# Attention scores taken once, query-major, with the probabilities transposed on TensorE and the causal mask added by VectorE

## The reference

```python
q = proj(Wq); k = proj(Wk); v = proj(Wv)          # B, 16 heads, 512 tokens, 32 features
scores = (einsum('bhnd,bhmd->bhnm', q_r, k_r) + einsum('bhnd,bhmd->bhnm', q_i, k_i)) / sqrt(16)
scores = where(tril(512, 512), scores, -inf)
probs = softmax(scores, axis=-1)
out = concatenate([probs @ v_r, probs @ v_i], -1)
x = x + reshape(out) @ Wo
```

## Time and profile before

| | |
|---|---|
| median of 3 runs | 826.6 us (825.58 to 826.87) |
| profiled execution | 829.26 us, its span 827.4 us |
| TensorE busy | 759.1 us (92%) |
| VectorE busy | 628.8 us (76%) |
| ScalarE busy | 402.8 us (49%) |
| GpSimd busy | 489.6 us (59%) |
| TensorE clock granted, mean | 0.971 |

### The profile page before, as it was taken

How to read it: one execution, slowest core, us unless ns; L and a number is a source line. 1 busy time by engine, 2 the same in 40 slices (tenths; PEclk the granted TensorE clock), 3 DMA queues, 4 the chain that set the end, 5 groups by cost and what they waited for, 6 DMA issues and landing times.

```text
span 827.4 us, 15883 instructions
## 1 busy us (share of the span) xinstructions
PE 759.1 (92%) x5563; PEld 520.8 (63%) x5563; DVE 628.8 (76%) x1225; ACT 402.8 (49%) x760; POOL 489.6 (59%) x452
## 2 busy tenths in 40 slices
PE   3688999999999999999999999999999998998997
PEld 2565655765566556666666666665766564587995
DVE  2544555457768998899879987999798879789873
ACT  5114555555555566545646573647464546541111
POOL 5000000031966799678958786878787888976541
PEclk9658999999999999999999999999999999999997
DMA  5886656866686668566646675667566760100001
GB/s 180 111 105 82 98 78 84 135 84 84 84 135 78 90 84 134 70 91 107 90 94 90 103 93 100 90 104 95 76 87 107 100 93 8 58 14 8 32 14 38
DMA packets 47980, 70.54 MB, mean 85 GB/s; under 512 B 4897, under 2 KB 22578, under 8 KB 47922
## 3 DMA queue, kind: packets, MB, share of 16 engines
q1 hardware_dynamic: 46898, 69.52, 56.1%
q10 hardware_dynamic: 1024, 0.26, 0.1%
HBM read 14.98 MB, written 4.19 MB: 23 GB/s over the span
## 4 chain that ended last, share of the span: by engine, by line
PE 58%; DMA 15%; DVE 13%; POOL 5%; issue 4%; ACT 2%; SPq 1%; DVEq 0%; ACTq 0%; POOLq 0%
PE misc L518 21%; DMA stack_k<-k_lo 14%; PE exp_bank L518 14%; PE acc_bank L518 9%; PE max_bank L518 9%; PE sum_bank L518 3%; POOL prod L1570 3%; DVE neg_max L1201 2%; DVE seg_max L1201 2%; DVE x L1296 2%; SPq L449 1%; POOL prod L311 1%; DVE head_scores L1213 1%; DVE head_out L1213 1%; DVE ln_raw L1179 1%
## 5 line engine op out<-in xcount | busy, mean ns | idle before, releaser
L927 ACT ACTIVATE probs<-exp_bank 128x512 f32<-128x512 f32 x320 | 188.4, 592 | 204.0 <-PE exp_bank L518 201.1
L1201 DVE TENSOR_REDUCE neg_max<-max_bank 128x1 f32<-128x512 f32 (+1 forms) x192 | 130.6, 683 | 93.0 <-PE max_bank L518 92.4
L1570 POOL TENSOR_TENSOR prod<-head_probs,ctx_sb 128x256 f32<-128x256 f32 (+1 forms) x100 | 185.1, 1882 | 2.2 <-POOL head_probs L1565 0.5
L518 PE MATMUL max_bank<-stack_k,stack_q 96*128 96x384 f32 (+3 forms) x512 | 158.2, 372 | 17.2 <-DMA stack_k<-k_lo 9.1
L518 PE MATMUL acc_bank<-probs,values 128*32 128x512 f32 (+3 forms) x1024 | 157.6, 445 | 4.6 <-ACT log_sum L938 2.6
L311 POOL TENSOR_TENSOR prod<-x1n,ctx_sb 128x256 f32<-128x256 f32 (+1 forms) x104 | 158.4, 1554 | 4.3 <-ACT x1n L887 4.3
L518 PE MATMUL sum_bank<-probs,ones 128*32 128x512 f32 (+3 forms) x1024 | 156.9, 442 | 0.0
L518 PE MATMUL exp_bank<-stack_q,stack_k 97*128 97x384 f32 (+3 forms) x512 | 150.0, 355 | 2.1 <-DVE wf_lo L1171 1.3
L1512 POOL TENSOR_TENSOR ln_var<-ln_mv,eps 128x4 f32<-128x4 f32 x21 | 4.5, 213 | 198.3 <-DVE ln_mv L1187 198.3
L518 PEld LDWEIGHTS exp_bank<-stack_q,stack_k 97*128 97x128 f32 x512 | 84.1, 194 | 56.2 <-issue 28.2
L1201 DVE TENSOR_REDUCE seg_max<-max_bank 128x4 f32<-128x512 f32 x128 | 86.7, 682 | 28.2 <-PE max_bank L518 27.0
(11 more groups left out here) (181 smaller groups left out, 1360.2 us busy)
## 6 DMA issues: line engine op xcount, KB each, us to landing
stack_q<-q_hi SPq DMA_DIRECT2D x64, 256.0 KB, 5.6
stack_k<-k_hi SPq DMA_DIRECT2D x64, 256.0 KB, 9.6
stack_q<-q_lo SPq DMA_DIRECT2D x32, 256.0 KB, 7.0
stack_k<-k_lo SPq DMA_DIRECT2D x32, 256.0 KB, 10.7
x_in<-in_x SPq DMA_DIRECT2D x9, 512.0 KB, 4.7
ctx_sb<-in_ctx SPq DMA_DIRECT2D x32, 128.0 KB, 3.3
x<-in_x SPq DMA_DIRECT2D x7, 512.0 KB, 10.1
out<-y_sb SPq DMA_DIRECT2D x5, 512.0 KB, 3.3
```

The costliest lines, as they stand in the source:

```text
L518: return nc.tensor.matmul(*args, **kw)
L927: nc.scalar.activation(probs[:, (UNITS * g + n) % PTR, :], exp_bank[n % 2][:, :], ACT.Exp, scale=SCALE).then_inc(exp_done, 1)
L1201: vec.tensor_reduce(o, v, axis=AX_X, op=ALU.max, negate=True).then_inc(max_taken, 1)
L1570: last = gp.tensor_tensor(pv_prod[:, COFF[j]:COFF[j + 1]].rearrange("p (q d k) -> p q d k", q=4, k=keys), head_probs[:, 4 * j:4 * j + 4, N ...
```

## The change

Stages B and C become one. Scores are computed once, query-major, 96 rows, no mask matmul, into three rotating banks (`score_bank`). VectorE takes a unit strip by strip with tensor_tensor_reduce: it adds a bf16 causal mask, writes the masked scores back to the bank, and keeps the smallest (q carries the factor -SCALE, so this is the negated maximum). ScalarE takes Exp strip by strip with scale -1, that minimum as a bias on every partition, and an accumulated row sum. TensorE transposes the four 128-column blocks of the unit into one of two turn banks, three units later (LAG = 3), ScalarE copies them to probs_t, and `attend` runs once for a group, four heads side by side, with the values alone. The row sums come from ScalarE; VectorE inverts them (`invert_sums`), ScalarE widens them (`widen_inverses`), four matmuls with the identity turn them (`spread_inverses`), and `normalise` multiplies. The matmuls with ones, Ln, the two Exp(-log), the turning of the maxima and its DMA are gone. Stage A is now one group ahead (it was three), with two slots; the batch loop is written out whole, without registers. The work of the head attention, the other layer norms, the feed-forward and the tail stays, some of it at another unit n.

```diff
-    SLOTS = 4
+    SLOTS = 2
-    PTR = 4
+    RING = 4
+    LAG = 3
...
-        max_bank = [psum(f"max_bank{n}", [P, T]) for n in range(2)]
-        exp_bank = [psum(f"exp_bank{n}", [P, T]) for n in range(2)]
+        score_bank = [psum(f"score_bank{n}", [P, T]) for n in range(3)]
+        turn_bank = [psum(f"turn_bank{n}", [P, T]) for n in range(2)]
...
-            return {"C": group(0), "B": group(2), "A": group(3), "M": group(1), "N": group(-1)}
+            return {"C": group(0), "A": group(1), "N": group(-1)}
...
+            def score_unit(n, slot):
+
+                wait(pe, exp_done, n_unit.up() - 3)
+                bank = score_bank[(n_unit.total - 1) % 3]
+                for h, blk, at, width in QUERY_UNITS[n]:
+                    last = mm(bank[:, at:at + width], stack_q[0:STACK, slot, h, blk * P:(blk + 1) * P],
+                              stack_k[0:STACK, slot, h, 0:width], start=True, stop=True, skip_group_check=True)
+                last.then_inc(scored, 1)
+
+            def turn_unit():
+
+                pe.wait_ge(exp_done, n_turned.up())
+                wait(pe, probs_kept, n_turned.total - 2)
+                unit = n_turned.total - 1
+                for j in range(NT):
+                    last = nc.tensor.transpose(turn_bank[unit % 2][:, j * P:(j + 1) * P],
+                                               probs[:, unit % RING, j * P:(j + 1) * P], ident[:, :])
+                last.then_inc(turned, 1)
+
+            def attend(group):
+
+                pe.wait_ge(probs_kept, UNITS * n_group.up())
+                wait(pe, acc_saved, n_group.total - 1)
...
+                for k, (blk, row, c0, c1, q0) in enumerate(VALUE_PARTS):
+                    for h in range(G):
+                        last = mm(acc_bank[h * D:(h + 1) * D, q0:q0 + c1 - c0], values[:, group, blk, h * D:(h + 1) * D],
+                                  probs_t[:, h, row, c0:c1], start=(k == 0), stop=(k == len(VALUE_PARTS) - 1),
+                                  skip_group_check=True)
...
+            def spread_inverses():
+
+                pe.wait_ge(inv_spread, n_group.total)
+                bank = take(1, attn_ready, r_attn)
+                for t in range(NT):
+                    last = mm(bank[:, t * P:(t + 1) * P], inv_wide[:, t, :], ident[:, :], start=True, stop=True)
...
+            def exponential(n, group):
+
+                act.wait_ge(max_taken, n_unit.up())
+                unit = n_unit.total - 1
+                wait(act, turned, n_unit.total - RING)
...
+                for h, blk, at, width in QUERY_UNITS[n]:
+                    last = nc.scalar.activation(probs[:, unit % RING, at:at + width],
+                                                score_bank[unit % 3][:, at:at + width], ACT.Exp,
+                                                bias=neg_max[:, ring, h, blk:blk + 1], scale=-1.0,
+                                                accum_out=row_sum[:, ring, h, blk:blk + 1])
+                last.then_inc(exp_done, 1)
...
+                for h, blk, at, width in QUERY_UNITS[n]:
+                    v = bank[:, at:at + width]
+                    last = vec.tensor_tensor_reduce(v, v, causal[:, T - width:T], 1.0, 3.0e38, ALU.add, ALU.min,
+                                                    neg_max[:, ring, h, blk:blk + 1])
+                last.then_inc(max_taken, 1)
```

More of the change, by code:

```diff
@@ L32, with __init__ @@
 class Count:
-    def __init__(self, turn, per_batch):
-        self.turn, self.per_batch, self.total = turn, per_batch, 0
+    def __init__(self):
+        self.total = 0
     def up(self, n=1):
         self.total += n
-        return self.now()
+        return self.total
     def now(self, back=0):
[L46 to L78, removed]
+        return self.total - back
 def wait(eng, sem, value):
-    if not isinstance(value, int) or value > 0:
+    if value > 0:
         eng.wait_ge(sem, value)
[L87 to L95, removed]
 def decoder_layer(nc, x, ctx_in, wq, wk, wv, wo, ffn_w, ffn_bias, ffn_a, ffn_b, out):
@@ L833, in _ @@
             pe.wait_ge(const_ready, 1)
-            turn.batches(pe, body, N_BATCH)
+            for i in range(-1, N_BATCH):
+                body(i)
             pe.wait_ge(setup_act, 2)
-            attend((8, 9), NG - 1, UNITS * (NG - 1))
+            for n in range(LAG):
+                turn_unit()
+            attend(NG - 1)
+            spread_inverses()
             last_projection_most()
@@ new lines, in keep_turned @@
+            def keep_turned(n):
+                act.wait_ge(turned, n_kept.up())
+                unit = n_kept.total - 1
+                if n == 0:
+                    wait(act, pv_done, unit // UNITS)
+                src = turn_bank[unit % 2][:, :]
+                place = turned_place(n)
+                if n < 2 * G:
+                    src = src.rearrange("p (b q) -> p b q", q=P)
+                else:
+                    src = src.rearrange("p (h b q) -> p h b q", b=2, q=P)
+                copy(place, src).then_inc(probs_kept, 1)
@@ L923, in body @@
                         if st["C"]:
-                            act.wait_ge(exp_scored, n_exp.up())
-                            wait(act, pv_done, n_exp.now(PTR) if turn.reg is not None or n_exp.total > PTR else 0)
-                            nc.scalar.activation(probs[:, (UNITS * g + n) % PTR, :], exp_bank[n % 2][:, :],
-                                                 ACT.Exp, scale=SCALE).then_inc(exp_done, 1)
+                            exponential(n, st["C"][1])
+                        if (i, g) == (-1, 3) and n == 3:
+                            other_weights()
@@ L1448, in _ @@
             last.then_inc(w_lo_ready, 1)
-            turn.batches(dve, body, N_BATCH)
+            for i in range(-1, N_BATCH):
+                body(i)
+            invert_sums(NG - 1)
             end_vector_scores(2)
-            last_normalise()
+            normalise(NG - 1)
             end_first_tile()
```

601 lines of the change are left out of this document (243 added, 358 removed).

## The result

The changed kernel takes 928.87 us (median of 4 runs, 927.21 to 929.92), the kernel before 826.15 in the same session: a ratio of 1.124, 95% interval 1.122 to 1.126. That is 103 us slower. The forecast was 848 with a range of 803 to 910, so the sign was right and the size far off.

A forecast was written before the change was run, and what follows sets the result against it. TensorE bounds the kernel, VectorE close behind. Start 32.5, batches 0 and 1 80 and 82, five batches 467.5, last 82, final units 3 and tail 101.7 sum to 848.7, taken as 848 us; range 803 to 910.

The forecast's parts named there:

- the sign: Whole kernel: slower, chance 0.68; faster 0.27, same 0.05.
- I leave VectorE about the idle time it has now: VectorE in a middle batch: idle time stays near 10.3 us, rounded to 9.8, giving 93.5 us instead of 86.2.
- Before, a late Exp did not hold up VectorE's maxima: Scores before the change: a late Exp left VectorE's maxima undelayed; afterwards late waits go round the engines; no size given.
- VectorE's 83.7 us: VectorE's work in a middle batch: 75.9 us less 28.3 removed, plus strips, read-outs and inversions; bounds 78.6 and 95.2.
- The extra eight microseconds: VectorE in a middle batch: the added eight microseconds come from cutting units into strips, not from the mask itself.
- ScalarE's 78 us: ScalarE's work in a middle batch: 32.0 us removed; copies, strip exponentials and row sums added; between 68 and 92.
- TensorE's 72.7: TensorE's work in a middle batch: 83.0 us, minus 29.9 removed, plus 19.6 for transposes and small matmuls.
- Start and light batches: Span's start: 32.5 us to the first score, 26 us lead gone; batches 0 and 1 take 80 and 82 us.
- The ring as forecast: Rival: engines wait in one ring of scores, exponentials and transposes, VectorE bound; about 848 us; chance 0.40.
- ScalarE joins the bound: Rival: row sums cost a full small instruction; ScalarE 89 to 92 us, batch 102, total 905; chance 0.20.
- The gain case: Rival: VectorE's read-outs hide and bank slack suffices; batch 83.5 us, total 783; decides at 89 a batch; chance 0.28.
- The clock rival: Rival: waits in every batch put TensorE at its lower clock half the time; 955 us; chance 0.12.

The follow-up runs named there:

- d1: Changed kernel with four moves: coefficients a group later, transposes ahead of the projection, inverses spread a unit later, attend behind unit 3's transposes; 829.10 us, ratio 0.999.
- b2: Changed kernel with three moves: coefficients a group later, transposes ahead of the projection, inverses spread a unit later; 839.38 us, ratio 1.009.
- the run with whole banks: Changed kernel with each unit's bank taken whole, one strip a unit; 910.49 us, ratio 1.097.
- the fifth buffer: Changed kernel with four moves of instruction order, and five probability buffers in place of four; 829.40 us, ratio 0.997.
- the mended kernels: Changed kernel with three moves of instruction order (839.38 us, ratio 1.009), or with attend behind unit 3's transposes as a fourth (824.93 us, ratio 0.994).
- c4: Kernel before with VectorE's next-input statistics in later units and GpSimd's coefficients in the same group, ahead of the head attention's products; 859.41 us, ratio 1.031.

## Why the prediction was wrong

The sign was right largely by luck: the forecast had it above all from 8 us more work on VectorE in a batch, and VectorE's work did not grow. The size failed at one step.

- **The step that failed** is "I leave VectorE about the idle time it has now": 9.8 us a batch. It was 29.8, and with it a middle batch took 104.9 us, not 93.5. In d1, with the single places mended, it was 10.6 in the batch at full clock: the term was right for the rings and missed the places. The sentence ahead of it, that the longest stretches of other work are shorter than the slack and "the ring should not stall at every unit", looked only at the ring. Three single places, each a step with a late input and something urgent queued behind it, hold 37 + 31 + 20 = 88 us of the 103 (b2 measured them taken together, 89.5). The order of the lists was there to be read before the run: for each moved step, where its input is made in the new order, and what stands behind it. I priced operations and skipped moved steps.
- **"Before, a late Exp did not hold up VectorE's maxima"** was a wrong reading of the list: a score for exp_bank that waits for exp_done stands ahead of the next score for max_bank on TensorE, as the order rows of the kernel before show. The kernel before had such a way round too.
- **VectorE's 83.7 us** was too high: 75.1. The strips with their read-outs cover 32.7 us where 35.1 was forecast. The reductions that went covered 27.3, not 25.6. The additions of head_out fell from 3.9 to 1.7 us a batch, which no term had. These make 6.3 of the 8.6 us; the rest was not traced. "The extra eight microseconds" for the strips were 2.8 on VectorE by the run with whole banks. So the forecast 93.5 for a batch came from too much work and too little waiting.
- **ScalarE's 78 us**: 75.2. Exponentials with row sums cover 37.2 us, forecast 37. **TensorE's 72.7** was right at full clock: 72.9 busy in d1's batch at 1.00. In the changed kernel it was 78.2, at a mean clock of 0.93.
- **Start and light batches.** The first Exp came at 33.83 us (forecast 34, before 58.38): the lead was lost as said. From one copy of acc_sb to the same one a batch later, the first two batches took 93.8 us (66.32 to 160.12) and 97.7 (to 257.84), not 80 and 82, since the waits of each group are there from the start. The forecast had counted batch 0 from its first score, so its 80 and the 93.8 are not the same stretch.
- **The rivals.** The ring as forecast (0.40) did not come: the single places outweighed it, and the fifth buffer gave nothing. "ScalarE joins the bound" gave 905 and the right neighbourhood by the wrong mechanism. The gain case (0.28) had its condition right: it decides at 89 us a batch, and at 88.3 and 89.0 us the mended kernels end at 1.009 and 0.994 of the kernel before.
- **The clock rival** (0.12) was half right. The clock did leave 1.00 in every middle batch, mean 0.93 to 0.96, and in the mended kernels too, 0.92 to 1.00. It fell behind waits: once behind the 6.54 us, and at 469.8 us behind 4 us in which TensorE was busy 1.60 (first row). In c4, the old design, it fell in the middle batches with the one wait put in, so transposes are not needed for it. Between 515 and 530 us TensorE ran 26 transposes among its 94 matmuls, with idle time too, at 1.00 (second row):

```profile
466.00:470.00 4.00, 1.60 (x7) 0.90 (x7) 2.40 (x10) 4.00 (x13) 4.00 (x2) 0.97 0.00 0
515.00:530.00 15.00, 10.95 (x94) 8.00 (x93) 11.32 (x36) 12.61 (x33) 11.17 (x11) 1.00 0.57 96
```

The Trainium skill, TensorE: Matmul & The Clock Gate, Part 4 (PE-mode transpose), says that the full clock does not engage for transposes. This row does not bear it out for a list in which scores and other matmuls stand between them, and nor does the whole batch of d1 at 1.00, with its 160 transposes; a stretch of transposes alone is in no run here.

What stays open: the last 10 us or so of the 103 went only with `attend` moved, and which wait it freed was not isolated. Of the 88 to 89 us of the mended kernel's batch some 3 go with the clock. At full clock it takes 85.8, with VectorE busy 75.2, as long as the kernel before (84 to 87, VectorE 75.9 in the batch of rows 2): TensorE's relief of 10 us gave nothing. It fits that VectorE's list is what both wait for, but no run took enough of its work away to show it.

## What to carry to other kernels

When a change reorders hand-written instruction lists, go through every moved step and ask three things ahead of all prices: in which unit of the new order is its input made, what is queued behind it on its engine, and who waits for that. In the trace, divide a wait's total by its count: a few long waits with one count per batch, or one per group, are a place that one line can mend, and such waits add up (37, 31 and 20 us here). Busy sums of 75 us in a batch of 105 make order the first suspect, whatever design they belong to; mend the order before the design is judged. And before a run with less work is read as "work does not count", read in its trace how much work it took away.

## What the runs showed of the hardware

Each accumulated result is an instruction of its own on both engines. The rows of the changed kernel, by line and shape (busy us, mean ns of one):

```profile
L1099 DVE CUSTOM_DVE_ANT_0 score_bank<-score_bank,causal 128x512 f32<-128x512 f32 x128 | 88.6, 693 | 41.4 <-PE score_bank L453 41.3
L1099 DVE DVE_READ_ACCUMULATOR2_ANT neg_max<- 128x1 f32 x512 | 73.4, 143 | 0.0
L1099 DVE CUSTOM_DVE_ANT_0 score_bank<-score_bank,causal 128x128 f32<-128x128 f32 x128 | 42.6, 333 | 0.0
L819 ACT ACTIVATION_READ_ACCUMULATOR probs<-score_bank,neg_max 128x1 f32 x512 | 110.3, 215 | 0.0
```

On VectorE a 384-wide operation starts at 536.91 us, its read-out and the next operation both at 537.38: the read-out's 143 ns lie beside that one. On ScalarE a read-out has a record of 215 ns; one starts at 463.25, the next exponential at 463.35. Leaving 64 of them out took 5.5 us off ScalarE's busy time in a batch, 0.09 each. An operation of 128 columns takes 333 ns, one of 512 takes 693: three quarters of the columns gone save about half.

The addition of head_out took 1190 ns on average before and 566 after, the same instruction on the same operands, now mostly beside other work of GpSimd's, or none. No run was made on what slowed it.
